# The largest weight of a head taken three heads ahead, and the turn from projections to attention reordered, in a fused transformer block on one core

## The reference

```
h = layernorm(x)
q, k, v = h @ Wq + bq, h @ Wk + bk, h @ Wv + bv        # 512 -> 4096 each
q, k = rms_norm(q) * gq, rms_norm(k) * gk              # over all 4096, per token
per batch and head (32 heads of 128):
    o = softmax(q @ k.T / sqrt(128)) @ v
x = x + layernorm(concat(o) @ Wo + bo)
z = layernorm(x)
x = x + layernorm(z @ W_base.T + b_base + 2 * sum over 8 experts of w_e * (z @ A_e.T) @ B_e.T)
```

## Time and profile before

| | us |
|---|---|
| three runs | 1146.56, 1146.83, 1148.07; median 1146.83 |
| the profiled execution | 1145.05 |
| its span, first to last instruction | 1143.1 |
| PE busy / DVE / ACT / POOL | 1075.6 / 798.8 / 723.9 / 686.2 |
| mean granted clock of PE | 0.977 of full |

### The profile page before, as it was taken

One profiled execution on the slowest core, in us unless ns is written; L12 is line 12 of the kernel. 1 busy time (PEld: TensorE's weight loads), 2 busy tenths in 40 slices (PEclk: granted clock), 3 DMA queues, 4 the chain that ended last, 5 costly groups with the idle time before them and its releaser, 6 DMA issues.

```text
span 1143.1 us, 19469 instructions
## 1 busy us (share of the span) xinstructions
PE 1075.6 (94%) x5708; PEld 577.3 (50%) x5708; DVE 798.8 (70%) x1802; ACT 723.9 (63%) x1427; POOL 686.2 (60%) x545
## 2 busy tenths in 40 slices
PE   5899999999997857999999999999999999999896
PEld 2444444444443534555555555555555555555385
DVE  7466656666655555777777777777777777777886
ACT  2565565565665366767776777677767777776532
POOL 1566656656657563766666666666666666664423
PEclk9899999999998888999999999999999999999899
DMA  5466566566564538787766666757666667776701
GB/s 205 152 217 221 194 209 211 198 216 201 195 229 128 197 82 197 176 180 171 194 175 172 177 174 177 189 159 191 178 170 177 173 174 192 160 173 128 197 1 74
DMA packets 312705, 199.47 MB, mean 174 GB/s; under 512 B 275168, under 2 KB 279392, under 8 KB 312544
## 3 DMA queue, kind: packets, MB, share of 16 engines
q1 hardware_dynamic: 312672, 199.06, 63.0%
HBM read 96.24 MB, written 35.68 MB: 115 GB/s over the span
## 4 chain that ended last, share of the span: by engine, by line
PE 59%; DMA 16%; ACT 9%; DVE 7%; issue 4%; POOL 2%; SPq 2%; ACTq 0%; DVEq 0%; POOLq 0%
PE ps L1040 19%; PE ps L1041 19%; PE ps L1042 19%; DMA qk_top_scratch<-qk_top 8%; DMA qk_tops<-qk_top_scratch 5%; ACT squares L780 4%; ACT qk_out L778 2%; ACT wa_hi L742 1%; DVE qk_out L1524 1%; ACT q_s L776 1%; DMA vo_top_scratch<-top_v 1%; DVE stats L1344 1%; DVE qk_most L1429 1%; ACT pair_q L894 1%; SPq L405 1%
## 5 line engine op out<-in xcount | busy, mean ns | idle before, releaser
L1680 DVE TENSOR_SCALAR_CACHE_REDUCE ps<-ps,score_down 128x512 f32<-128x512 f32 x256 | 177.6, 755 | 98.1 <-PE ps L1042 97.9
L1694 DVE SCALAR_TENSOR_TENSOR pair_q<-ps,row_inv,pair_q 128x512 f16<-128x512 f32 x256 | 174.5, 744 | 71.5 <-ACT pair_q L894 57.3
L1040 PE MATMUL ps<-xh,wa_hi 128*128 128x512 f16 x512 | 197.1, 385 | 16.6 <-DVE wa_lo L1444 14.5
L1041 PE MATMUL ps<-xl,wa_hi 128*128 128x512 f16 x512 | 197.0, 385 | 0.0
L885 ACT ACTIVATE ps<-ps,neg_max 128x512 f32<-128x512 f32 x256 | 168.1, 657 | 44.9 <-DVE ps L1680 44.8
L1042 PE MATMUL ps<-xh,wa_lo 128*128 128x512 f16 x512 | 196.4, 384 | 0.0
L894 ACT ACTIVATE pair_q<-ps,row_inv 128x512 f16<-128x512 f32 x256 | 155.2, 689 | 31.7 <-DVE row_inv L1687 20.6
L650 POOL CAST oth<-o_t 128x512 f16<-128x512 f32 x62 | 37.9, 611 | 223.9 <-ACT o_t L870 223.9
L555 POOL TENSOR_TENSOR qk_out<-q_s,qk_out 128x512 f16<-128x512 f32 x64 | 74.3, 1161 | 126.2 <-ACT qk_out L778 126.2
L1042 PE MATMUL ps<-wv_hi,xl 128*128 128x256 f16 x512 | 140.3, 274 | 0.0
L1041 PE MATMUL ps<-wv_lo,xh 128*128 128x256 f16 x512 | 140.3, 274 | 0.0
(11 more groups left out here) (180 smaller groups left out, 2298.4 us busy)
## 6 DMA issues: line engine op xcount, KB each, us to landing
q_k_scratch<-qk_out SPq DMA_DIRECT2D x32, 1024.0 KB, 4.9
qk_in<-q_k_scratch SPq DMA_DIRECT2D x64, 512.0 KB, 3.3
wa_stage<-w_qk SPq DMA_DIRECT2D x32, 512.0 KB, 5.9
u_stage<-w_vo SPq DMA_DIRECT2D x32, 512.0 KB, 5.9
wv_stage<-w_vo SPq DMA_DIRECT2D x16, 512.0 KB, 4.2
wo_stage<-w_vo SPq DMA_DIRECT2D x16, 512.0 KB, 4.6
qk_tops<-qk_top_scratch SPq DMA_DIRECT2D x30, 128.0 KB, 4.2
y<-x SPq DMA_DIRECT2D x8, 256.0 KB, 5.3
```

The source lines that it names most:

```text
L1040: pe.matmul(outp, lhs[0], rhs[0], start=first, stop=False)
L1041: pe.matmul(outp, lhs[0], rhs[1], start=False, stop=False)
L1680: dve.tensor_scalar(ps[:, SCORE + i, :], ps[:, SCORE + i, :], score_down[:, sl, i:i + 1], None, ALU.mult, ALU.min, accum_out=neg_max[:, sl ...
L1694: dve.scalar_tensor_tensor(out=pair_q[:, 1, i, :], in0=ps[:, SCORE + i, :], scalar=row_inv[:, sl, i:i + 1], in1=pair_q[:, 0, i, :], op0=AL ...
```

## The change

It moves work and adds little:

- `largest_qk` runs for head h+3 instead of h+2, and behind `next_factors(h+1)`. `qk_tops` has two buffers. SP loads weights of head h+4, loads the tops of h+2 and then stores those of h+3.
- The loop of phase A ends one turn earlier for DVE and ACT, and the last four heads are written out: two units of Wv and Wo each, the value factors within head 28's part.
- The start: moments of x ordered anew, the sum of head 0's tops behind all four turnings, `low_wa(2)` behind the last `store_k` of head 1, the eight loads of bo moved from the start into SP's part of the first four attention steps.
- `item` on ACT squares first and makes queries after it; in the turn the seventh product's queries come behind the spreading.
- The turn: `spread` takes the root's column, broadcast, as an operand against the identity, and `diagonals` is gone. The second V item moves behind the first scores; `attend(0)` behind the scores of step 2. DVE makes the low halves of the first two pairs of Wv and of the first of Wo, which POOL made between its parts of the first steps. The last queries' low halves come behind the first two steps' keys on POOL. The two last stores of q and k come behind the first turnings on SP's queue.

The diff, cut to its core:

```diff
@@ SP, phase A
-            def load_tops(h):
+            def load_tops(h, par):
                 sp.wait_ge(qk_top_stored, 16 * (h - 1))
-                sp.wait_ge(qk_most_ready, h)
-                sp.dma_start(qk_tops[:, :, :], qk_top_scratch[bass.ds(h, 1)].broadcast_to(
+                sp.wait_ge(qk_most_ready, h - 1)
+                sp.dma_start(qk_tops[:, par], qk_top_scratch[bass.ds(h, 1)].broadcast_to(
                     [P, P, 2])).then_inc(qk_tops_loaded, 16)
-                if load:
-                    sp.wait_ge(wa_lo_ready, 2 * h)
-                    load_wa(h + 3, (o + 3) % 4)
-                store_tops(h + 2, par)
-                load_unit(h - 1, 1 - par, h - 1)
-                load_tops(h + 2)
+                if not last or o < 0:
+                    sp.wait_ge(wa_lo_ready, 2 * h + 2)
+                    load_wa(h + 4, o % 4)
+                if last:
+                    load_unit(29 + 2 * o, 1, 29 + 2 * o)
+                else:
+                    load_unit(h - 1, 1 - par, h - 1)
+                load_tops(h + 2, par)
+                if not last or o < 1:
+                    store_tops(h + 3, 1 - par)
+                if last and o < 1:
+                    load_unit(30 + 2 * o, 0, 30 + 2 * o)
                 store_qk(h, par, 2 * h + 2)
...
@@ PE, the turn
-                pe.wait_ge(diag_ready, b + 1)
-                pe.matmul(ps[:, bank, :], ones[:, :], factors(b), start=True, stop=True).then_inc(rms_spread, 1)
+                pe.wait_ge(rms_ready, b + 1)
+                for k in range(TB):
+                    col = NT * b + TB + k
+                    ins = pe.matmul(ps[:, bank, k * P:(k + 1) * P], rms[:, col:col + 1].broadcast_to([P, P]),
+                                    ident[:, :], start=True, stop=True)
+                ins.then_inc(rms_spread, 1)
...
-            column_sums(1, 2)
-            v_item(0, 2, OB)
+            column_sums(1, YB + 1)
...
             scores(0, 0, first=True)
+            v_item(0, 2, OB)
             spread(1, YB)
             pe.wait_ge(qk_lo_ready, 2)
             scores(1, 1)
             values(0, 1, 0, 1)
-            pe.wait_ge(rms_row_ready, 2)
-            attend(0, 0, 0)
             pe.wait_ge(qk_lo_ready, 3)
             scores(2, 2)
+            attend(0, 0, 0)
             values(0, 2, 0, 2)
...
@@ DVE, phase A
-                if top:
-                    largest_qk(h + 2, par, (o + 2) % 4, 16 * (i + (o + 2) // 4 + 1))
+                if last and o == -2:
+                    largest_value()
                 next_factors(h + 1, 1 - par)
+                if last and o == 0:
+                    value_factors()
+                    value_biases()
+                if not last or o < 1:
+                    largest_qk(h + 3, 1 - par, (o + 3) % 4, 16 * (i + (o + 3) // 4 + 1))
                 low_wa(h + 1, 1 - par, (o + 1) % 4)
...
@@ DVE, before the first scores
+            low_wo(0)
+            low_wo(1)
...
@@ POOL, the first steps
             scale_k(0, 2)
             low_k(2, 2)
             scale_k(0, 3)
-            split_wv(1, 1, 0, 1)
-            split_wv(1, 1, 2, 2)
             low_k(3, 3)
             split_o(0, 0)
             scale_k(1, 0)
-            split_wo(0, 0, 0, 3)
-            split_wo(0, 0, 1, 4)
             low_k(0, 4)
```

More of the change, by code:

```diff
@@ L908, in step @@
                 for i in range(TB):
[L909 removed]
+                    high_halves(n, sl, i)
                 if value:
@@ L912, in step, with first_steps @@
                 weights()
+            def first_steps():
+                for i in range(TB):
+                    exponentials(0, 0, i)
+                for i in range(TB):
+                    high_halves(0, 0, i, True)
+                spread(1, YB)
+                evacuate_v(2, 2, OB)
+                for i in range(TB):
+                    exponentials(1, 1, i)
+                high_k(2, 2)
+                for i in range(TB):
+                    high_halves(1, 1, i)
+                high_k(3, 3)
+                evacuate_v(3, 4, VB)
+                for i in range(TB):
+                    exponentials(2, 0, i)
+                output(0, 2)
+                high_k(0, 4)
+                for i in range(TB):
+                    high_halves(2, 0, i)
+                evacuate_v(4, 6, VB)
+                wo_part(1, 1, 0, None)()
+                step(0, 3, 0, wo_part(1, 1, 1, None))
             def wo_part(pair, slot, h, used):
@@ L953, in _ @@
             act.wait_ge(v_bias_ready, 1)
-            step(0, 0, 0, second_wv, first=True, output=False, value=False)
-            step(0, 1, 0, first_wo, output=False)
-            step(0, 2, 0, nothing)
-            step(0, 3, 0, second_wo)
+            first_steps()
             pair_of_heads(1, 1)
@@ L1590, in phase_a @@
                 dve.wait_ge(k_cols_ready, 3 * h + 3)
+                if last:
+                    largest_of_unit(28 + 2 * o, 0, 16 * (15 + o))
                 store_k(par, 0, h, 4 * h + 2)
-                largest_of_unit(h - 2, par, 16 * (2 * i + o // 2))
+                if last:
+                    largest_of_unit(29 + 2 * o, 1, 16 * (15 + o))
+                else:
+                    largest_of_unit(h - 2, par, 16 * (2 * i + o // 2))
                 store_k(par, 1, h, 4 * h + 4)
-            with dve.Fori(1, PAIRS // 2) as i:
+            with dve.Fori(1, PAIRS // 2 - 1) as i:
                 for o in range(-2, 2):
                     phase_a(i, o)
+            for o in range(-2, 2):
+                phase_a(PAIRS // 2 - 1, o, last=True)
             def mean_squares(b, bank):
@@ L1714, in step @@
                 if value:
-                    split_v(n + 2, 2 * ((s + 1) % 4), VB)
+                    split_v(n + 2, 2 * ((s + 1) % 4), OB if first else VB)
                 if down:
+                    if first:
+                        dve.wait_ge(rms_ready, 2)
                     scores_down(n + 1, 2 * p + (s + 1) % 2 + (2 if s == 3 else 0), 1 - sl, (s + 1) % 4 // 2)
-            step(0, 0, 0, first=True, value=False, rows=False)
-            out_factors()
-            for s in range(1, 4):
-                step(0, s, 0, rows=False)
+            for s in range(4):
+                step(0, s, 0, first=s == 0, rows=False)
             dve.wait_ge(y_down_ready, 1)
+            dve.wait_ge(y_set, 16 * NT)
             for s in range(4):
```

311 lines of the change are left out of this document (157 added, 154 removed).

## The result

| set of runs | kernel before, us | changed kernel, us | ratio, 95% interval |
|---|---|---|---|
| first (4 runs each) | 1147.45 | 1129.84 (1125.91 to 1133.04) | 0.9845 [0.9812, 0.9877] |
| second (9 and 5) | 1147.32 | 1128.72 | 0.9836 [0.9814, 0.9858] |
| fifth (17 and 5) | 1160.16 | 1132.42 | 0.9759 [0.9738, 0.9781] |

Faster, by 17.6 us (1.5%) where 35.1 were forecast: 1129.84 lies outside 1102 to 1121.

A forecast was written before the change was run, and what follows sets the result against it. TensorE, busy 94% of the span, was taken as the bound, with only gaps and half-clock stretches to win. Loop 7.5 (after head 29), start 0.5 and turn 27.1 sum to 35.1 us: 1111.7 us, range 1102 to 1121.

The forecast's parts named there:

- The loop: Projection heads: taking the largest three heads ahead makes TensorE the bound at 10.38 us a head; 9.2 us won.
- keys-to-keys chain: Loop: path from one stored key to the next loses the 1.21 us largest, falling from 10.0 to 8.8 us.
- the longer trip of the tops: Loop: tops get one head more to go to DRAM and back; 8.0 us per head, under 10.38.
- Head 29: Loop's end: low weights stand behind value factors that wait for the value tops' load; -1.7 us, bounds 0 and -4.
- "I add nothing" for the shared port: Loop: low halves waiting on GpSimd for SBUF's port cost at most 3.2 us, within 3.8 in hand; no loss added.
- The start: Before head 2: reordered moments and loads against later first product and low weights; net +0.5 us, bounds -2 and +4.
- The first product: Start: begins some 0.6 us later, since the sum over first tops now follows all four turnings on TensorE.
- The turn: Head 30's start to the fourth step's scores: 61.4 us against 88.5, 27.1 won; bounds 54 and 72.
- both falls: Turn: half clock after the second column sum and in step 2's wait, 1.7 us each, 3.4 in all.
- the high halves of the third step: Turn: they stand behind one of the keys that GpSimd scales after its output split; 0.7 us.
- The 13.51 us stop: Turn: TensorE's wait for turned probabilities, behind wo's load waiting for GpSimd's low halves, goes as DVE makes them earlier.
- B: Rival: loop stays bound by late tops' loads, or turnings stand behind bo and stores; 1117 to 1126 us, chance 0.17.

The follow-up runs named there:

- The repair: Changed kernel plus head 2's low halves earlier, value factors later, eight-byte top stores, GpSimd's head 29 sum after head 31's low halves: 1112.74 us, 1114.14 in the fifth set.

## Why the prediction was right or wrong

**The loop, 9.2 us won: right.** The keys-to-keys chain without its 1.21 us and the longer trip of the tops did what they should: no DVE wait for tops, heads 10.36 apart, alone as well as in the change. My price was that of one set of runs; where landings are longer it is 15.6 us (309.3 - 293.7).

**Head 29, -1.7 (bounds 0 and -4): the step that failed.** With its half clock it cost 10.4 us. I priced the tops' load behind a store of 1 MB and had the store of four-byte rows in my own rows, 10.2 us, but took it as something that only its reader waits for. In the order before, nothing was issued close behind it; in the new one three loads are. The unit behind it is then late by 5 us, and the keys, the tops' load and the value factors stand in line behind that unit. The two together are the step: the run without the stores gave back 9.4 us, 7.1 of it at head 29 by the traces, the one with the factors moved 5.8.

**"I add nothing" for the shared port: wrong.** For the loop proper it held; there two halves take 1.9 to 2.1 us and fit into the lead. At heads 2, 29 and 31 no lead was left, and there the rule that I had weighed and put aside is the price: 5.6 against 1.4, 3.7 against 1.4, 3.7 to 4.5 against 1.4. Only the first two came with the change; head 31's halves took 3.92 before it too. I bounded a half at 2.36 us by the earlier trace rows; the change moved halves to where two additions stand without a break, and 2.8 was seen. I also misread that row: the longest half is not the last, at 360.2, but the one ahead of it, begun at 357.93 beside the second of GpSimd's two additions; the last took 1.64. Read so, the row is the wait for the rest of one addition, and no bound.

**The start, +0.5 (bounds -2 and +4): -6.1, outside.** The first product, 0.6 us later forecast, was 0.3. The wait for the second batch's xl ended at 36.09, 2.6 us earlier than before, but TensorE had stopped 3.98 us there, and 13 matmuls at half clock, 2.8 us, brought the eighth product's end to 49.4 (49.2 before), not 46: a fall that I had not priced. My terms were also added wrongly: 51.0 - 49.5 less 1.7 is -0.2, not +0.5. The low halves stood behind the last key of head 1, as I said, and took 5.6, not 1.5 to 2.5. Head 2 began at 57.1, not 49.5.

**The turn, 61.4: 65.7, inside its bounds.** The scores begin 35.4 us in, forecast 31.2. Of the 4.2 more, 0.7 is at head 31, 1.85 ahead of the first column sum, where I had none, and 1.7 a fall of the clock behind that sum; I had put both falls later. The 1.85 is released by the wait of ACT for head 29's store, but it is not shown that the small store costs the turn anything: in the run without it the column sum began no earlier. From there it took 30.3 us where I had 26.8 and 3.4 for two falls, 30.2, and that it fits is luck: the steps between DVE's first scalings are 8.9, 8.8 and 12.9 us, so the falls cost almost nothing on the path and the third step 4.2 us. For the high halves of the third step I put 0.7. In their place DVE waited 5.19 us for ACT, which waited 3.27 for the key that GpSimd scales after the first output. The repair does not touch this, its turn takes 66.2, and no run was made on it. The 13.51 us stop was the right cause at the right price.

**The rivals.** B, 1117 to 1126, came nearest and was still 4 us too low, and its causes were not these: neither the tops' loads in the loop nor bo in the turn. It should have said "a slow store delays what is issued behind it". With the three places repaired the kernel takes 1112.7 to 1114.1, near where I had put the change. The loop's gain was sized well (292.0 us for 292.3); the turn's was put 4.8 us too high, and the losses at the seams were missed.

## What to carry to other kernels

A change that takes away slack moves the cost to the first and last turns of the loop; go through those turns instruction by instruction, with what the other engines do in the same microseconds, and price a two-input DVE operation beside GpSimd by GpSimd's instruction and not by its own. A store of four bytes from each partition is to be suspected of holding up the DMA issued close behind it until it lands, on whichever queue; look at the landings of its neighbours and not only at who waits for it. And a kernel whose loop waits for a round trip through DRAM can differ from one set of runs to the next (1147 to 1162 us here); the one that covers it differed little (1129 to 1132), so the gain is to be measured beside its own before.

## What was not expected of the hardware

A store of 128 rows of four bytes took 7.1 to 11.1 us to land; one of 128 rows of eight bytes, in the same two places, 4.5 to 7.2. Loads and stores of 512 KB or 1 MB issued within 3 us behind the first landed in 9 to 13 us instead of 5 to 7, also when it stood in another engine's queue. Of the stores of 1 MB ahead of it, those 0.4 to 1 us ahead were never late (4.3 to 5.0 us), and head 29's, 2 us ahead, always was (9.3 to 12.0). The landing times of the same loads differ between sets of runs by 0.3 to 0.4 us (medians of the tops' loads and stores), and the loop of the kernel before by 9.5 us with them. Why a row of four bytes is slower than one of eight, and why three DMAs without such a store near them landed late once, no run here shows; nor was it tried to spread the rows in DRAM, or to make the sum over partitions on TensorE so that no store is left.
